# Eight cores, a linear-attention layer and a ternary-weight FFN: the weight pieces get one pool of eighteen buffers, twelve of them keep their piece, and VectorE shares the sums

## The chip, the cores and the metric

The program runs on all 8 cores of one Trainium2 chip. Each core computes one batch element of 4096 rows on its own, with its own copy of the weights. The time is device microseconds of the slowest core; a result is a median of runs. "Span" is the time from the first to the last instruction of one profiled execution.

## The reference, cut to what matters

One layer: linear attention with chunks of 64, then a feed-forward part whose two weight matrices are quantized to -1, 0, 1.

```python
x = x + layernorm(attn(layernorm(x), W_qkv, W_o))     # x: 8 x 4096 x 1024
x = x + layernorm(ffn(layernorm(x), w1, b1, w2, b2, gamma, beta))

def weight_quant(w):                       # w1: 4096 x 1024, w2: 1024 x 4096
    scale = 1.0 / clip(mean(abs(w)), EPS)
    return clip(round(w * scale), -1, 1), scale
def qlinear(x, w, b):                      # rows of x quantized to 8 bits
    return (xq @ wq.T) / (sx * sw) + b
def ffn(x): h = layernorm(x) * gamma + beta
            return qlinear(gelu(qlinear(h, w1, b1)), w2, b2)
```

The threshold of a matrix needs the mean of all its magnitudes, so no element can be quantized before the whole matrix has been read once. The matrix is then needed a second time.

## The kernel before

The 4096 rows are 32 tiles of 128. There are two phases, and in both each engine has its program written out by hand, with semaphores between the engines.

**Attention phase.** A loop over i from -1 to 31. In iteration t, TensorE does K, Q and V of tile t+1, scores and outputs of tile t and ends with `out_proj(t)` (L403), 16 matmuls of 512 columns. ScalarE turns PSUM results out (`k_out`, `q_out`, `y_out`, `kf_out`) and takes norms (`ln2_sd`, needed by VectorE's `x1`). VectorE does `ln1`, `x1` (L523, which empties the PSUM pair that the next scores use), `ln3`, `masks` (L541, before TensorE's `attend`), `k_sums`, `v_scaled` (L558, empties the pair that the next K uses). The normalized rows `h1t` are turned by a DMA transpose issued from SP (L980); there is one `h1t` buffer, so ScalarE's `h1` of a tile waits for the transpose of the tile before. Tiles are normalized two at a time, in even iterations. In the last two iterations VectorE also prepares FFN rows (`front_a`, `front_b`, L601 to L631), for which gamma and beta must be loaded (L1127, L1128, the last DMAs of POOL before the end of this phase).

**The weights, in the background of that phase.** w1 and w2 are cut into 32 pieces each of 128 x 1024 float32 (512 KB). Each piece is loaded twice: once for its sum of magnitudes ("sum"), once for quantization ("quant"). The list `plan[t]` says which of the 128 steps belong to iteration t: cost 1 for a sum, 1.75 for a quant, spread over iterations 0 to 29, in even iterations a little less. A sum is one ScalarE activation with accumulation (L887). A quant is: POOL's `below` (L1102, writes `lt`, two buffers), VectorE's `quant_piece` (L569, writes `wqt`, four buffers), a DMA transpose from SP into `w1p` or `w2p` (L987, L991). On ScalarE the first sum of an iteration stands before `y_out`, the rest at the iteration's end, ahead of the next `ln2_sd`. On VectorE, in odd iterations, the first quant stands before `masks`, the second before `v_scaled`, the rest behind it; in even ones the first before `v_scaled`, the rest behind it.

POOL issues the loads (L1123) in the order of the steps, at most four in flight, each after its buffer is free. Buffers before: eight in the space of `w1p` (`pc1`) for the 32 sums of w1, eight in the space of `w2p` (`pc2`) for the next 64 steps, then four for the rest (`pc` and two of `pc2`), two for the last six. For a quant POOL's order is `below(q-2)`, load of q, `below(q-1)`, load of q+1: a piece is asked for two steps ahead.

**FFN phase.** For each tile `ffn1` (L427, fp8 weights, 64 matmuls), then `ffn2` (L439, 64 matmuls), with gelu on ScalarE and quantization on VectorE.

## Time and profile before

| | |
|---|---|
| median of 3 runs | 1606.2 us (1605.7 to 1608.01) |
| the profiled execution's time | 1602.83 us |
| its span on the slowest core (core 2) | 1601.3 us, 1591.7 to 1601.3 over the cores |
| PE / DVE / ACT / POOL busy | 91% / 70% / 41% / 18% |
| attention phase, to the end of the last `out_proj` | to 685 us |
| FFN loop after it | from 709 us to the end |
| HBM read / written by the core | 119.03 MB / 33.55 MB |

Busy shares are means over two phases with different limits, so they are read by stage. TensorE is the engine with the most work in both; the time between two `out_proj` of neighbouring iterations shows what an iteration took.

### The profile page before, as it was taken

Reading aid. Unit: us, or ns where it says so; the run is one execution under the profiler, and the core shown is the slowest. Engines: PE = TensorE matmul, PEld = TensorE weight load, DVE = VectorE, ACT = ScalarE, POOL = GpSimd, SP = SyncE. Lnnn points to the kernel's source line nnn. Section 1 sums busy time; section 2 is a strip of 40 time slices with the busy share of each in tenths; the row PEclk is TensorE's granted clock in tenths of the full one; section 3 lists DMA queues with packets and bytes.
Section 4 is the critical chain, followed back from the end, with each engine's and each line's share of the span. In section 5 each row is a group of like instructions: output and inputs, shape, how many; then the busy total and the mean of one; then the engine's idle time right before and its main releaser. Section 6 shows DMA issues by size and latency. Waiting matters only on the chain.

```text
span 1601.3 us, 26580 instructions; the slowest of 8 cores (1591.7 to 1601.3 us)
## 1 busy us (share of the span) xinstructions
PE 1459.8 (91%) x8948; PEld 723.0 (45%) x8948; DVE 1116.3 (70%) x1861; ACT 662.8 (41%) x1057; POOL 282.3 (18%) x211
## 2 busy tenths in 40 slices
PE   0488599999999998689999999999999999999997
PEld 0245355655555555334444444444444444444443
DVE  3755356677777876676777767777677776767764
ACT  1078477677555655333323232232322323223231
POOL 1111124555667775000000000000000000000000
PEclk9989899999999999999999999999999999999999
DMA  9968868988889786243342543424334243342422
GB/s 192 294 162 250 195 160 203 215 228 230 188 188 214 197 180 159 90 89 79 81 100 61 107 74 81 100 61 111 71 82 98 60 111 71 89 92 60 103 52 66
DMA packets 285045, 209.94 MB, mean 131 GB/s; under 512 B 246632, under 2 KB 248680, under 8 KB 284912
## 3 DMA queue, kind: packets, MB, share of 16 engines
q1 hardware_dynamic: 261776, 131.16, 36.7%
q0 software_dynamic: 23136, 77.08, 18.1%
q8 instruction: 74, 1.21, 0.4%
q14 instruction: 59, 0.48, 0.1%
HBM read 119.03 MB, written 33.55 MB: 95 GB/s over the span
## 4 chain that ended last, share of the span: by engine, by line
PE 66%; DMA 12%; issue 7%; ACT 4%; DVE 4%; DVEq 3%; POOL 2%; SPq 2%; ACTq 1%; POOLq 0%
PE pz L439 28%; PE pp L427 27%; DMA pc<-w 7%; PE pp L317 4%; DMA h1f<-h1t 3%; PE pp L335 2%; PE pp L403 2%; POOL lt L1102 2%; DMA kst<-w_qkv 1%; PE pp L418 1%; ACT pc L887 1%; SPq L1007 1%; DVEq L725 1%; DVEq L512 1%; DVE wqtp L569 1%
## 5 line engine op out<-in xcount | busy, mean ns | idle before, releaser
L427 PE MATMUL pp<-w1p,xq1f 128*128 128x512 fp8e4 x2048 | 457.0, 381 | 0.0
L439 PE MATMUL pz<-w2p,xq2f 128*128 128x512 fp8e4 x2048 | 447.1, 379 | 0.0
L439 PEld LDWEIGHTS pz<-w2p,xq2f 128*128 128x128 bf16 x2048 | 200.4, 98 | 241.6
L427 PEld LDWEIGHTS pp<-w1p,xq1f 128*128 128x128 bf16 x2048 | 195.8, 98 | 243.9 <-issue 19.9
L638 DVE TENSOR_REDUCE st<-gsb 128x1 f32<-128x1024 f32 x128 | 152.6, 1214 | 130.6 <-ACT gsb L895 130.4
L901 ACT ACT_TABLE_LOAD x31 | 39.8, 1283 | 469.5 <-DVE st L677 469.5
L1102 POOL TENSOR_SCALAR lt<-pc,st 128x1024 bf16<-128x1024 f32 x64 | 192.5, 3008 | 143.6 <-DMA pc<-w 83.2
L895 ACT ACTIVATE gsb<-pp,st 128x1024 f32<-128x1024 f32 x128 | 142.1, 1110 | 104.5 <-PE pp L427 98.7
L317 PE MATMUL pp<-wk,h1f 128*128 128x512 bf16 x512 | 121.2, 389 | 68.9 <-DMA h1f<-h1t 33.2
L317 PE MATMUL pp<-wv,h1f 128*128 128x512 bf16 x512 | 125.8, 390 | 15.7 <-ACT kt L838 12.6
L1123 POOL DMA_DIRECT2D pc<-w x128 | 82.8, 647 | 215.7 <-ACT pc L887 115.0
L403 PE MATMUL pp<-wo,yf 128*128 128x512 bf16 x512 | 115.7, 379 | 1.2 <-ACT yf L867 1.2
L569 DVE SCALAR_TENSOR_TENSOR wqtp<-pc,st,lt 128x1024 fp8e4<-128x1024 f32 x64 | 85.7, 1346 | 37.9 <-POOL lt L1102 37.8
L317 PEld LDWEIGHTS pp<-wk,h1f 128*128 128x128 bf16 x512 | 50.7, 100 | 130.9 <-issue 77.5
L660 DVE TENSOR_SCALAR xq2t<-gsb 128x1024 bf16<-128x1024 f32 x128 | 88.8, 694 | 19.4 <-issue 1.5
L541 DVE TENSOR_TENSOR scT<-pp,mask 128x1024 bf16<-128x1024 f32 x64 | 75.3, 1218 | 35.9 <-PE pp L346 35.9
L655 DVE TENSOR_SCALAR gsb<-gsb,st 128x1024 f32<-128x1024 f32 x128 | 95.8, 749 | 2.8 <-issue 0.4
L317 PEld LDWEIGHTS pp<-wv,h1f 128*128 128x128 bf16 x512 | 47.3, 100 | 67.9 <-issue 22.7
L670 DVE SCALAR_TENSOR_TENSOR zb<-pz,st,b2b 128x512 f32<-128x512 f32 x64 | 47.9, 748 | 39.6 <-PE pz L439 39.6
L403 PEld LDWEIGHTS pp<-wo,yf 128*128 128x128 bf16 x512 | 48.7, 98 | 54.2 <-issue 1.3
L838 ACT CAST kt<-pp 128x512 bf16<-128x512 f32 x64 | 35.8, 582 | 76.8 <-PE pp L317 76.7
L335 PE MATMUL pp<-h1f,wqa 128*128 128x256 bf16 x512 | 60.2, 277 | 7.6 <-DMA h1f<-h1t 7.6
(114 smaller groups left out, 1511.5 us busy)
## 6 DMA issues: line engine op xcount, KB each, us to landing
pc<-w POOLq DMA_DIRECT2D x128, 512.0 KB, 5.9
xs<-x SPq DMA_DIRECT2D x32, 512.0 KB, 5.7
x1s<-xs SPq DMA_DIRECT2D x32, 512.0 KB, 4.6
xs<-x1s SPq DMA_DIRECT2D x32, 512.0 KB, 3.6
out<-xs SPq DMA_DIRECT2D x32, 512.0 KB, 3.1
wost<-w_o POOLq DMA_DIRECT2D x8, 512.0 KB, 49.3
kst<-w_qkv SPq DMA_DIRECT2D x8, 512.0 KB, 19.5
wv<-w_qkv POOLq DMA_DIRECT2D x1, 2048.0 KB, 31.6
```

Of the source, the lines that this page charges most:

```text
L317: mi = PE.matmul(half(n, h), lhsT=hf[:, kk, :], rhs=wt[:, kk, h * 512:(h + 1) * 512], start=(kk == 0), stop=(kk == 7))
L335: mi = PE.matmul(pair(n)[:, m * 256:(m + 1) * 256], lhsT=wt[:, kk, m * 128:(m + 1) * 128], rhs=hf[:, kk, :], start=(kk == 0), stop=(kk == ...
L403: mi = PE.matmul(half(n, h), lhsT=yf[:, kk, :], rhs=wo[:, kk, h * 512:(h + 1) * 512], start=(kk == 0), stop=(kk == 7))
L427: mi = PE.matmul(half(n, h), lhsT=xf[:, kk, :], rhs=w1q[:, kk % 4, c0:c0 + 512, kk // 4], start=False, stop=(kk == 7), skip_group_check=True)
L439: mi = PE.matmul(PZ[:, h * 512:(h + 1) * 512], lhsT=xq2f[:, t % 2, kk, :], rhs=w2q[:, kk % 16, h * 512:(h + 1) * 512, kk // 16], start=(kk ...
L569: V.scalar_tensor_tensor(out=wqt[:, j % 4].rearrange("p n e -> p e n"), in0=piece_buf(q)[0].rearrange("p (e n) -> p e n", e=2), scalar=c1( ...
L638: V.tensor_reduce(out=c1(amq, s), in_=gsb[:, s * 1024:(s + 1) * 1024], axis=AX.X, op=ALU.max, apply_absolute_value=True)
L655: V.tensor_scalar(out=g, in0=g, scalar1=s2, scalar2=M32, op0=ALU.mult, op1=ALU.add)
L660: V.tensor_scalar(out=xq2t[:, s * 1024:(s + 1) * 1024], in0=g, scalar1=M32, scalar2=None, op0=ALU.subtract).then_inc(s_xq2, 1)
L895: A.activation(out=gsb[:, s * 1024:(s + 1) * 1024], in_=pair(n)[:], func=AF.Gelu, scale=c1(dq1, t % 2)).then_inc(s_fr[n % 3], 2)
L1102: GP.tensor_scalar(out=lt[:, j % 2], in0=buf, scalar1=c1(nth, p[1]), scalar2=None, op0=ALU.is_lt).then_inc(s_lt, 1)
L1123: GP.dma_start(out=dst, in_=piece_src(p)).then_inc(s_ld, 16)
```

## The change

- **Layout.** `w1p` and `w2p` are laid out piece by piece: a transposed piece is 1024 bytes in a row of each partition. The moving operand of the FFN matmuls is then 4 blocks of 128 columns, where it was 512 columns in a row. TensorE waits for w2's transposes only before the first `ffn2`.
- **Buffers.** One pool of 18: two of `pc`, eight of `pc1`, eight of `pc2`. A buffer in the space of `w1p` or `w2p` may be used until the first piece that is written over it is quantized. Seven pieces of w1 and five of w2 stay in their buffer between sum and quant: 116 loads, where there were 128.
- **Order and time.** The pieces that stay are summed last. w2 is quantized in its plain order. The steps are spread over iterations 0 to 30, with 1.6 for a quant.
- **Sums.** VectorE takes 27 of the 64 sums (`piece_vsum`, a reduction of magnitudes), 17 of them of w1; ScalarE keeps 37.
- **POOL.** Before the step at place q of the list, POOL issues all loads whose buffer's last use is at place q-2 or earlier, then does `below` if the step is a quant.

```diff
-    w1p = at("w1p", O_W1, [4, HID], BF16)
-    w2p = at("w2p", O_W2, [16, D], BF16)
+    w1p = at("w1p", O_W1, [NWP, 4, 128], BF16)
+    w2p = at("w2p", O_W2, [8, 16, 128], BF16)
...
+    gap, hold = 12, (7, 5)
+    order = [list(range(hold[k], NWP)) + list(range(hold[k])) for k in range(2)]
...
-    line += [("quant", 1, 4 * c + b) for b in range(4) for c in range(8)]
-    cost = {"sum": 1.0, "quant": 1.75}
+    line += [("quant", 1, j) for j in range(NWP)]
+    cost = {"sum": 1.0, "quant": 1.6}
+    first, last = 0, T - 2
...
+    def on_dve(p):
+        return p[0] == "sum" and (p[2] < hold[p[1]]
+                                  or place[p] < NWP + gap and place[p] % 5 in (1, 3))
...
+    bufs = ([pc[:, k] for k in range(2)] + [pc1[:, k] for k in range(8)]
+            + [pc2[:, k] for k in range(8)])
+    covered = ([4 * NWP] * 2 + [place[("quant", 0, 4 * k)] for k in range(8)]
+               + [place[("quant", 1, 4 * k)] for k in range(8)])
+    held = [-1] * 10 + [8] * 8
...
+        z = min((b for b in own if end < covered[b]), key=lambda b: held[b])
...
-                                       rhs=w1q[:, kk % 4, c0:c0 + 512, kk // 4],
+                                       rhs=w1q[:, c0 // 128:c0 // 128 + 4, kk % 4, :, kk // 4],
...
-                                   rhs=w2q[:, kk % 16, h * 512:(h + 1) * 512, kk // 16],
+                                   rhs=w2q[:, 4 * h:4 * h + 4, kk % 16, :, kk // 16],
...
+        def piece_vsum(p):
+            buf, s_ld, landed = piece_buf(p)
+            V.wait_ge(s_ld, landed)
+            V.tensor_reduce(out=c1((acc1, acc2)[p[1]], p[2]), in_=buf, axis=AX.X, op=ALU.add,
+                            apply_absolute_value=True).then_inc(s_vabs, 1)
...
+            if p[2] % 4 == 0 and sums_under(p[1], p[2]) > 0:
+                SP.wait_ge(s_abs, sums_under(p[1], p[2]))
...
+        def load(n):
+            p = loads[n]
+            buf, s_ld, _ = piece_buf(p)
+            if n >= 4:
+                GP.wait_ge(piece_buf(loads[n - 4])[1], piece_buf(loads[n - 4])[2])
+            o, used = prior[p]
...
+            if used and pieces[o][0] == "quant":
+                GP.wait_ge(s_q, nqua[o] + 1)
...
+            GP.dma_start(out=buf, in_=piece_src(p)).then_inc(s_ld, 16)
...
         for q, p in enumerate(pieces):
...
+            while n < len(loads) and prior[loads[n]][0] <= q - 2:
+                load(n)
+                n += 1
+            if p[0] == "quant":
+                below(p)
```

## Rows read from the trace of the kernel before

**Rows 1.** Windows: the stages; time, busy of each engine, granted clock, DMA share, GB/s.

```profile
94.00:225.00 131.00, 105.12 (x871) 61.31 (x869) 59.10 (x107) 96.80 (x201) 21.41 (x36) 0.93 0.79 206
225.00:449.00 224.00, 214.72 (x1875) 128.25 (x1874) 161.75 (x251) 158.68 (x327) 119.54 (x81) 1.00 0.86 210
449.00:614.00 165.00, 151.28 (x1299) 90.03 (x1297) 128.15 (x187) 91.55 (x190) 110.13 (x58) 0.98 0.82 191
709.00:1602.00 893.00, 882.75 (x4210) 389.30 (x4208) 651.72 (x1139) 258.81 (x246) 0.00 (x0) 1.00 0.36 82
```

**Rows 2.** Timeline of PE: `out_proj` of iterations 0, 6, 13, 14, 19, 28, 30.

```profile
93.96 3.62 PE L403 MATMUL pp<-wo,yf 128*128 128x512 bf16 x16
...
224.77 3.62 PE L403 MATMUL pp<-wo,yf 128*128 128x512 bf16 x16
...
345.44 3.62 PE L403 MATMUL pp<-wo,yf 128*128 128x512 bf16 x16
361.77 3.62 PE L403 MATMUL pp<-wo,yf 128*128 128x512 bf16 x16
...
448.97 1.24 PE L403 MATMUL pp<-wo,yf 128*128 128x512 bf16 x5
...
614.00 3.62 PE L403 MATMUL pp<-wo,yf 128*128 128x512 bf16 x16
...
651.40 3.62 PE L403 MATMUL pp<-wo,yf 128*128 128x512 bf16 x16
```

**Rows 3.** Groups by line: costs of the operations that the change touches.

```profile
L1102 POOL TENSOR_SCALAR lt<-pc,st 128x1024 bf16<-128x1024 f32 x64 | 192.5, 3008 | 143.6 <-DMA pc<-w 83.2 <-DVE wqtp L569 59.6
...
L887 ACT ACTIVATE pc<-pc 128x1024 f32<-128x1024 f32 x64 | 67.0, 1050 | 0.0
...
L610 DVE TENSOR_REDUCE st<-h 128x1 f32<-128x1024 f32 x32 | 39.0, 1220 | 2.4
```

**Rows 4.** Timelines around iteration 5: POOL, ACT, then PE.

```profile
175.61 0.70 POOL L1123 DMA_DIRECT2D pc<-w  x1 [2.63 <-DMA pc<-w]
178.85 1.24 ACT L811 ACTIVATE h1t<-xs,st 128x1024 bf16<-128x1024 f32 x1 [11.27 <-DMA h1f<-h1t]
182.16 5.36 PE L317 MATMUL pp<-wk,h1f 128*128 128x512 bf16 x16 [9.85 <-DVE vt L558]
192.21 5.32 PE L335 MATMUL pp<-h1f,wqa 128*128 128x256 bf16 x32 [4.69 <-DMA h1f<-h1t]
```

**Rows 5.** One line's view: transposes of h1 (L980), then of xq2 (L1076), to landing.

```profile
DMA to landing us min/median/max: 3.0/5.3/16.9
...
DMA to landing us min/median/max: 3.0/3.4/5.0
```

**Rows 6.** Timelines, iterations 19 and 20: POOL, then DVE.

```profile
452.68 2.83 POOL L1102 TENSOR_SCALAR lt<-pc,st 128x1024 bf16<-128x1024 f32 x1 [3.23 <-DMA pc<-w]
455.68 2.82 DVE L569 SCALAR_TENSOR_TENSOR wqtp<-pc,st,lt 128x1024 fp8e4<-128x1024 f32 x1 [4.25 <-POOL lt L1102]
460.10 1.41 DVE L523 SCALAR_TENSOR_TENSOR xs<-pp,st,xs 128x512 f32<-128x512 f32 x2
```

**Rows 7.** Timelines, iteration 29 to the first FFN matmul: DVE, POOL, PE.

```profile
630.04 1.27 DVE L569 SCALAR_TENSOR_TENSOR wqtp<-pc,st,lt 128x1024 fp8e4<-128x1024 f32 x1
641.65 1.29 DVE L569 SCALAR_TENSOR_TENSOR wqtp<-pc,st,lt 128x1024 fp8e4<-128x1024 f32 x1 [4.67 <-POOL lt L1102]
652.73 1.16 DVE L601 SCALAR_TENSOR_TENSOR h<-xs,st,gam 128x1024 f32<-128x1024 f32 x1
638.64 2.84 POOL L1102 TENSOR_SCALAR lt<-pc,st 128x1024 bf16<-128x1024 f32 x1 [3.12 <-DMA pc<-w]
662.80 0.61 PE L418 MATMUL pp<-b1r,xq1f 4*128 4x512 bf16 x2 [7.78 <-DMA xq1f<-xq1t]
```

**Rows 8.** Landing: piece loads (L1123) from 600 to 640 us, then beta's.

```profile
DMA to landing us min/median/max: 4.4/5.4/6.6
...
bet<-beta POOLq DMA_DIRECT2D x1, 512.0 KB, 5.3
```

More of the change, by code:

```diff
@@ L222, in build @@
     s_S = sem("state_out")
[L223 to L226 removed]
+    s_pl = [sem(f"piece_loaded{i}") for i in range(18)]
+    s_abs, s_vabs = sem("piece_summed"), sem("piece_summed_by_dve")
+    s_lt, s_q = sem("piece_lt"), sem("piece_quantized")
     s_wtp = [sem(f"piece_transposed{i}") for i in range(4)]
@@ L253, in build @@
         spent += cost[p[0]]
-    last_sum = [max(i for i in range(T) if ("sum", k, NWP - 1) in plan[i]) for k in range(2)]
+    last_sum = [max(i for i in range(T) if ("sum", k, NWP - 1) in plan[i]
+                    or ("sum", k, hold[k] - 1) in plan[i]) for k in range(2)]
     assert all(p[0] == "sum" or last_sum[p[1]] + 2 <= i for i in range(T) for p in plan[i])
@@ L258, in build @@
     place = {p: q for q, p in enumerate(pieces)}
-    nsum = [sum(1 for p in pieces[:q] if p[0] == "sum") for q in range(len(pieces))]
-    nqua = [sum(1 for p in pieces[:q] if p[0] == "quant") for q in range(len(pieces))]
-    early = 3 * NWP
-    def piece_buf(q):
-        if q < NWP:
-            return pc1[:, q % 8], s_wl1[q % 8]
-        if q < early:
-            return pc2[:, q % 8], s_wld[q % 8]
-        z = (q - early) % 4 if q < early + 24 else (q - early) % 2
-        return (pc[:, z] if z < 2 else pc2[:, 4 + z]), s_wll[z]
@@ new lines, in build @@
+    nsum = [sum(1 for p in pieces[:q] if p[0] == "sum" and not on_dve(p))
+            for q in range(len(pieces) + 1)]
+    nvsum = [sum(1 for p in pieces[:q] if on_dve(p)) for q in range(len(pieces) + 1)]
+    nqua = [sum(1 for p in pieces[:q] if p[0] == "quant") for q in range(len(pieces) + 1)]
+    bufs = ([pc[:, k] for k in range(2)] + [pc1[:, k] for k in range(8)]
+            + [pc2[:, k] for k in range(8)])
+    covered = ([4 * NWP] * 2 + [place[("quant", 0, 4 * k)] for k in range(8)]
+               + [place[("quant", 1, 4 * k)] for k in range(8)])
@@ new lines, in build @@
+    held = [-1] * 10 + [8] * 8
+    count = [0] * 18
+    loads, where, prior = [], {}, {}
+    for p in pieces:
+        if p[0] == "quant" and p[2] < hold[p[1]]:
+            where[p] = where[("sum", p[1], p[2])]
+            continue
+        stays = p[0] == "sum" and p[2] < hold[p[1]]
+        end = place[("quant", p[1], p[2])] if stays else place[p]
+        own = range(2 + 8 * p[1], 10 + 8 * p[1]) if stays else range(18)
+        z = min((b for b in own if end < covered[b]), key=lambda b: held[b])
+        count[z] += 1
+        where[p] = (z, 16 * count[z])
+        prior[p] = (held[z], count[z] > 1)
+        held[z] = end
+        loads.append(p)
@@ L288, in q_of, with piece_buf, sums_under @@
+    def piece_buf(p):
+        return bufs[where[p][0]], s_pl[where[p][0]], where[p][1]
+    def sums_under(k, z):
+        under = [place[p] for p in pieces
+                 if p[0] == "sum" and not on_dve(p) and where[p][0] == 2 + 8 * k + z // 4]
+        return nsum[max(under)] + 1 if under else 0
     def q_of(t, j):
@@ L495, in pe_program @@
                 ffn1(t + 1, [2, 3])
+            if t == 0:
+                for k in range(4):
+                    PE.wait_ge(s_wtp[k], 16 * 2 * NWP // 4)
             ffn2(t)
@@ L574, in quant_piece, with take_piece @@
                                    saturate=False).then_inc(s_q, 1)
+        def take_piece(p):
+            if p[0] == "sum":
+                piece_vsum(p)
+            else:
+                quant_piece(p)
         def w_total(k):
-            V.wait_ge(s_abs, NWP * (k + 1))
+            V.wait_ge(s_abs, nsum[max(place[("sum", k, j)] for j in range(NWP)) + 1])
+            V.drain()
             V.tensor_reduce(out=c1(tot, k), in_=(acc1, acc2)[k], axis=AX.X,
@@ L743, in dve_program @@
                     w_total(k)
-            now = [p for p in plan[t] if p[0] == "quant"] if 0 <= t < T else []
+            now = [p for p in plan[t] if p[0] == "quant" or on_dve(p)] if 0 <= t < T else []
             if two:
@@ L766, in dve_program @@
             for p in now[done:done + 1]:
-                quant_piece(p)
+                take_piece(p)
             if u < T:
@@ L937, in act_program @@
                 gelu(0, 1)
-            now = [p for p in plan[t] if p[0] == "sum"] if t >= 0 else []
+            now = [p for p in plan[t] if p[0] == "sum" and not on_dve(p)] if t >= 0 else []
             for p in now[:1]:
```

87 lines of the change are left out of this document (29 added, 58 removed).

## The prediction

> **What bounds the kernel now.** I read the stages first [rows 1]. From 709 us TensorE is busy 882.75 of 893 us at full granted clock: the FFN loop is TensorE's own time, and only the speed of its matmuls can change it. Before that, from 94 to 225 us, TensorE is busy 105 of 131 us at a mean clock of 0.93, while ScalarE is busy 97; from 225 to 449 it is nearly full; from 449 to 614 it loses 14 us, with VectorE at 128 of 165. So what the change can win lies in the first and the third stretch of the attention phase.
>
> The steps between two `out_proj` say it more exactly [rows 2]. Iteration 14 took 361.77 - 345.44 = 16.33 us, the least that I saw, and several took just that: TensorE without a wait. Against it: iterations 1 to 6 took 224.77 - 93.96 = 130.8, six times 16.33 is 98.0, so 32.8 us are lost. Iterations 7 to 19: 224.2 against 212.3, 11.9 lost. 20 to 28: 165.0 against 147.0, 18.1 lost. 29 and 30: 37.4 against 32.7, 4.7 lost.
>
> The early loss has two parts. Iteration 5 alone was 18 us late. Before it POOL had asked for w2's first pieces into eight untouched buffers, four always in flight, to 175.61 [rows 4]. The h1 transposes beside them took up to 16.9 us where the median is 5.3 [rows 5]; ScalarE sat 11.27 us for the one `h1t` buffer, and TensorE 9.85 and 4.69 [rows 4]. The matmuls behind the waits are also slow: 16 of them in 5.36 us, where `out_proj` has 16 in 3.62. The rest, some 9 us in iterations 1 to 4, is ScalarE: five or seven sums of 1.05 us [rows 3] in each iteration, four to six of them ahead of `ln2_sd`, so `x1` and `k_out` come late.
>
> The loss of 20 to 28 is mostly of one kind [rows 6]: POOL waits for a piece that was asked for only two steps ahead (3.23 us), VectorE waits for POOL's `lt` (4.25), and `x1` of the next iteration starts at 460.10, some 9 us after its `out_proj` allowed it. `lt` waited 83.2 us for loads in all [rows 3].
>
> **The change part by part**, against the profiled execution of 1602.8 us; the median of the runs is 3.4 above it, and I carry the difference over.
>
> *Sums to VectorE, spread of loads (iterations 1 to 6).* ScalarE keeps 3, 4, 3, 3, 2, 1 sums in iterations 0 to 5, where it had 5, 7, 5, 7, 5, 7. `ln2_sd` then comes 2 to 5 us sooner. VectorE gets 17 reductions of w1, of about 1.22 us each (the magnitude maximum over the same shape, [rows 3]), 2 to 3 in an iteration of 16, 6 in iteration 5. VectorE is busy 59 of 131 us there [rows 1], so 21 us more fit: one in odd iterations lies ahead of `masks`, but `x1` has moved up by more. That takes away nearly all of the 9 us. The loads: walking the list, the untouched buffers are now met in groups of 10 at the start, 6 behind the sum at place 8 (iteration 1) and 2 behind place 18 (iteration 3), the last with four more whose buffers are free by then. So two bursts of about 9 loads stand where one of 13 stood, ending near the h1 transposes of iterations 2 and 4. The last four loads of a burst, 2 MB, need about 2 MB / 206 GB/s = 10 us at the stage's rate [rows 1], against the 5.3 us that a transpose may take. I take 3 us lost at the first burst, 6 at the second, 3 elsewhere, 12 in all: a gain of 32.8 - 12 = **20**. Bounds: 29 if the bursts do no harm (some 4 us of threshold and pairing waits stay), 5 if the transposes stall as before and only part of ScalarE's 9 us comes back.
>
> *Middle (7 to 19).* As many ScalarE sums per iteration as before; five VectorE sums for the kept w2 pieces fall into iterations 15 to 17, where VectorE then has 4, 3 and 5 pieces: about 16 us of work in the even one, just its length. Against this stand deeper loads. **0**, from -5 to +5: the loss there is 11.9, and either side can take some of it.
>
> *Deeper loads (20 to 28).* A load now goes out as soon as its buffer's last use is two places back, which puts it 2 to 8 places ahead of its quant up to place 121. `lt` then waits only for VectorE: the fourth piece of an odd iteration is ready about 0.5 + 0.8 + 3 us after the second is quantized, and VectorE gets to it after about 4. So the waits of [rows 6] go. Of 18.1 lost I leave 4 (slow h1 transposes, even iterations with three pieces): gain **14**, from 8 to 17.
>
> *The end of the list.* This is the part that costs. w2's transposes cover its buffers as they go, and the last pieces have only the two `pc` buffers and one more. The loads of places 124 to 127 find their buffer's last use exactly two places back, so they are issued at their own place, directly before `below` waits for them: nothing is fetched ahead. Before, at places 122 to 127, a `below` stood between. The list also ends one iteration later: 121 to 124 in iteration 29, 125 to 127 in iteration 30, where before there was none. Iteration 30 is also where VectorE, behind its last quant, prepares the first FFN rows, and TensorE already waits for these: its first FFN matmul comes at 662.80 after 7.78 us idle [rows 7].
>
> Let X be the end of iteration 29's second quant (630.04 + 1.27 = 631.3 before). Before, the rows were begun at 652.73 and the FFN at X + 31.5. After: the load of 124 waits for X, plus 0.5 to wake; landing takes 4.4 to 6.6 us, median 5.4 [rows 8]; I take 4.9, since one is in flight and not two; `below` takes 2.84 to 3.0 [rows 3, 7]. Four such steps follow each other on POOL: X + 0.5 + 4 x (4.9 + 2.9) = X + 31.7. Quant 127 ends at about X + 33. But gamma and beta are asked for only behind POOL's last `below`: + 0.6 for the first issue + 5.3 for beta to land [rows 8] = X + 37.6, which is later. From there the rows and their transpose take what they took, 662.80 - 652.73 = 10.1: X + 47.7. That is 16.2 later than X + 31.5. `masks(30)`, held up behind quant 125 by some 3 us, lies inside that wait. **Cost 16**, from 14 (landing 4.4) to 23 (landing 6.6). If it were covered by nothing else being late it would be zero, but TensorE was already idle at this place, so every microsecond counts.
>
> *Layout.* Zero for the transposes: turned rows with stepped destinations (h1) and with unbroken ones (xq2) both take 3.0 us at least [rows 5]. The Trainium skill, "DMA: Bandwidth & Descriptors", section "Latency and other measured facts", says that a transpose with a non-contiguous middle dimension runs at 261 GB/s where a contiguous one has 350 to 400; by that the pieces' transposes would be a third shorter. The rows above do not agree, and no wait for a piece's transpose is among them, so the sum is the same by either. For the FFN matmuls, no row has a moving operand in four blocks of 128. From below nothing excludes a cost; I take zero, because 64 matmuls' worth of stepped fp8 columns already run with TensorE always busy [rows 1]. A gain is excluded, since it is never idle there.
>
> 12 loads fewer, 6 MB of 119 and 12 issues of 0.65 us, are inside the terms above. SP's new waits for sums are long met; VectorE's added drain in `w_total` is one of two.
>
> **Sum:** -20 + 0 - 14 + 16 + 0 = -18. Profiled time 1602.8 - 18 = 1585; median 1606.2 - 18 = **1588**.
>
> **The rivals.**
> - *The transposes stall as before (0.15).* The DMA share is 0.79 already in this stretch [rows 1], and the same megabytes come sooner. Then the early gain is 5: -5 - 14 + 16 = -3, about 1603, at best just faster. The Trainium skill, same page, section "Issuing engines are not separate DMA queues", says that DMAs from all engines share 16 engines and interleave, so that a transpose is behind whatever POOL has asked for. The 16.9 us in [rows 5] agrees. The rule counts what is in flight, and that stays at four.
> - *VectorE becomes the bound (0.10).* It waits in order for pieces to land, ahead of `masks` and `x1`, and at 97% in iterations 16 and 17. Half of the early gain goes and 5 us in the middle: -10 + 5 - 10 + 18 = +3, about 1609. Against it: early loads run at least ten places ahead of their sum.
> - *The four-block operand slows the FFN (0.07), slower.* There are 63 x 64 = 4032 such matmuls in 893 us, 221 ns each. From 18 us / 4032 = 4.5 ns more (2%) the gain is gone; at 10 ns the time is 1588 + 40 = 1628. For it speaks only that no row shows such an operand; against it, that the blocks are still 256 bytes in a row.
> - *The end costs little (0.08).* If the last loads land in 4.4 and iteration 29 runs earlier than I allow, +12 and -32: about 1573. The chain on POOL speaks against less.
>
> **How the numbers follow.** My own case has 0.60, 1575 to 1600. A difference within 0.2% (3.2 us) can't be told from none here. Faster: 0.60 + 0.08 + two thirds of the first rival (0.09) + a third of the second (0.03) = 0.80. Within 0.2%: 0.05 + 0.03 = 0.08. Slower: 0.07 + 0.04 + 0.01 = 0.12. The range goes from 1571 (early gain 27, deeper loads 17, end 14: -30, with some room below) to 1607 (the first rival with an end of 20).
>
> **What would show it.** Right: iterations 1 to 4 at about 17 us, iteration 5 no longer 34; h1 landings at most 10 us; no wait of L569 for `lt` in iterations 20 to 28; piece loads of places 124 to 127 each followed by a wait of POOL for them, VectorE idle in iteration 30, and TensorE idle some 20 us before its first FFN matmul; the FFN loop as long as before. Wrong: an FFN loop longer than 893 us, transposes of 15 us beside bursts, or VectorE waiting for loads in iterations 1 to 5.

## The result, and the profile after

The changed kernel takes **1627.2 us** (median of 4 runs, 1625.0 to 1638.5), the kernel before, beside it, 1607.1 (4 runs, 1605.7 to 1608.1): a ratio of **1.014, 95% interval 1.0092 to 1.0188**. It is 20 us slower. The forecast was 1588, range 1571 to 1607: wrong in sign, and outside the range. The profiled execution took 1624.97 us.

In some executions half of the chip's cores run at a lower granted clock: such executions are left out of the times, and where it touched the profiled one (wait_seven_back and h1_turned_first, some of cores 4 to 7, 0.86 to 0.93 in the middle), the middle is read on cores 0 to 3. The kernel before took 1602.5, 1605.9 and 1603.0 us beside the three groups of experiments.

The page of the kernel after: the span, the engines' busy times, the traffic, both FFN matmuls, and POOL's `below`.

```profile
span 1623.4 us, 26481 instructions; the slowest of 8 cores (1609.6 to 1623.4 us)
...
PE 1460.7 (90%) x8884; PEld 726.6 (45%) x8948; DVE 1149.8 (71%) x1888; ACT 637.3 (39%) x1003; POOL 271.7 (17%) x199
...
HBM read 112.74 MB, written 33.55 MB: 90 GB/s over the span
...
L444 PE MATMUL pp<-w1p,xq1f 128*128 128x512 fp8e4 x2048 | 457.0, 382 | 0.0
L456 PE MATMUL pz<-w2p,xq2f 128*128 128x512 fp8e4 x2048 | 447.1, 380 | 0.0
...
L1135 POOL TENSOR_SCALAR lt<-pc,st 128x1024 bf16<-128x1024 f32 x64 | 188.5, 2946 | 44.5 <-DMA pc<-w 22.8
```

The wait of `below` for loads fell from 83.2 us [rows 3] to 22.8, and 6 MB less were read. The kernel is slower all the same. Windows of the kernel after, core 2, cut at the same `out_proj` as [rows 1]; columns as there.

```profile
94.00:225.00 131.00, 104.06 (x862) 61.25 (x872) 80.50 (x126) 79.24 (x163) 20.53 (x34) 0.90 0.79 196
225.00:467.00 242.00, 217.18 (x1835) 130.79 (x1860) 168.15 (x255) 149.23 (x308) 104.41 (x68) 0.96 0.73 177
467.00:617.00 150.00, 147.58 (x1285) 89.02 (x1302) 127.45 (x187) 92.66 (x191) 102.43 (x53) 1.00 0.79 187
617.00:704.00 87.00, 54.02 (x394) 29.15 (x395) 45.52 (x69) 29.02 (x56) 29.69 (x16) 0.84 0.42 107
704.00:1623.00 919.00, 906.84 (x4313) 399.39 (x4314) 672.17 (x1168) 268.91 (x260) 0.53 (x1) 1.00 0.37 83
```

ScalarE was relieved in the first stretch (79 us busy, 97 before [rows 1]) and the stretch is as long as it was. The second is longer with a clock of 0.96 where it was 1.00; the third is shorter; the fourth has TensorE busy 54 of 87 us. From the start of the last `out_proj` to the end of the span it is 919.1 us on core 2, before 919.7: the FFN part is as long as it was.

The yardstick for all that follows is the time between the starts of two `out_proj` in the timeline of PE, as in [rows 2], here as a mean over the 8 cores of each kernel's profiled execution. Kernels in which a stretch is untouched differ there by up to 3.5 us, 5 in the middle; a step ("step 9" is the time from `out_proj` of iteration 8 to that of iteration 9) is a mean of the 8 cores too.

| us, mean of 8 cores | 1 to 6 | 7 to 19 | 20 to 28 | 29 to 31 | start of last `out_proj` |
|---|---|---|---|---|---|
| before | 129.3 | 225.2 | 161.2 | 66.3 | 676.8 |
| after | 129.4 | 237.9 | 150.0 | 85.3 | 696.2 |
| forecast of the difference | -20 | 0 | -14 | +16 | -18 |
| measured | +0.1 | +12.7 | -11.2 | +19.0 | +19.4 |
| two_in_flight | 104.3 | 236.9 | 150.1 | 83.9 | 668.2 |
| two_in_flight_old | 119.3 | 232.3 | 160.3 | 66.2 | 671.0 |
| two_in_flight_not_shared | 113.0 | 233.6 | 151.6 | 85.9 | 678.5 |
| wait_seven_back | 129.3 | 232.6 | 149.6 | 85.8 | 690.7 |
| h1_turned_first | 131.6 | 239.1 | 148.9 | 83.5 | 696.4 |
| tail_prefetched | 132.8 | 241.4 | 150.1 | 75.0 | 693.5 |
| list_ends_at_29 | 132.0 | 240.3 | 159.3 | 75.6 | 701.9 |
| all_three_mended | 103.9 | 228.5 | 149.5 | 75.1 | 651.9 |
| mended_two_throughout | 106.8 | 223.5 | 151.7 | 74.9 | 649.8 |
| mended_threshold_odd | 106.1 | 231.3 | 151.1 | 74.1 | 656.1 |
| layout_only | 129.4 | 224.7 | 158.9 | 65.9 | 672.2 |
| old_list_to_30 | 112.2 | 222.2 | 157.1 | 78.4 | 663.1 |

**The first stretch.** Steps 1 to 6 took 16.3, 16.4, 29.2, 16.3, 30.8 and 20.4 us, where they were 17.8, 19.7, 19.0, 19.7, 31.6 and 21.3. Timelines of the kernel after, core 2: POOL's loads, then ScalarE, then TensorE.

```profile
111.85 2.23 POOL L1154 DMA_DIRECT2D pc<-w  x4 [4.93 <-ACT pc L918]
...
126.64 0.53 POOL L1154 DMA_DIRECT2D pc<-w  x1 [1.65 <-DMA pc<-w]
...
154.51 2.03 POOL L1154 DMA_DIRECT2D pc<-w  x3 [2.86 <-DVE st L586]
...
182.04 0.72 POOL L1154 DMA_DIRECT2D pc<-w  x1 [5.02 <-DMA pc<-w]
...
136.91 1.24 ACT L843 ACTIVATE h1t<-xs,st 128x1024 bf16<-128x1024 f32 x1 [12.19 <-DMA h1f<-h1t]
...
183.96 1.24 ACT L843 ACTIVATE h1t<-xs,st 128x1024 bf16<-128x1024 f32 x1 [13.95 <-DMA h1f<-h1t]
...
140.21 5.14 PE L334 MATMUL pp<-wk,h1f 128*128 128x512 bf16 x16 [10.87 <-DVE vt L578]
...
187.27 5.50 PE L334 MATMUL pp<-wk,h1f 128*128 128x512 bf16 x16 [12.71 <-DVE vt L578]
```

The h1 transposes issued at 118.89 and 163.68 us, inside the two bursts, landed after 17.9 and 20.2 us, with 3.4 and 3.8 piece loads in flight beside them on the mean (on the eight cores, 17.2 to 20.2 us). So the picture of [rows 4] is there twice. One line's view of the h1 transposes of the kernel after (L1011), issue to landing, from 60 to 130 and from 130 to 180 us:

```profile
DMA to landing us min/median/max: 3.4/5.9/17.9
...
DMA to landing us min/median/max: 3.1/11.7/20.2
```

**The middle.** Of its +12.7 us, 9.3 are step 9 (26.8, before 17.5) and 5.5 step 18 (21.8, before 16.3); others go up and down by up to 2.3. Waits of the kernel after, core 2, 222 to 467 us: in total, times, longest.

```profile
POOL pc L1154 <- DVE wqtp L594: 66.2, 14, 12.4
POOL pc L1154 <- ACT pc L918: 58.3, 9, 16.4
POOL pc L1154 <- DVE st L586: 11.2, 1, 11.2
...
PE pp L352 <- DMA h1f<-h1t: 18.4, 5, 7.2
```

Before, POOL's waits there were the 68.4 us of `below` for loads; to free a buffer it waited 10.8, and TensorE waited 0.2 for h1. Timelines of step 9 (core 2): POOL, VectorE, ScalarE, SP, TensorE.

```profile
262.42 0.70 POOL L1154 DMA_DIRECT2D pc<-w  x1 [11.17 <-DVE st L586]
263.16 2.85 POOL L1135 TENSOR_SCALAR lt<-pc,st 128x1024 bf16<-128x1024 f32 x1
...
260.66 1.20 DVE L586 TENSOR_REDUCE st<-pc 128x1 f32<-128x1024 f32 x1
...
263.78 1.23 DVE L578 TENSOR_TENSOR vt<-pp,st 128x1024 bf16<-128x1024 f32 x1
266.12 1.29 DVE L594 SCALAR_TENSOR_TENSOR wqtp<-pc,st,lt 128x1024 fp8e4<-128x1024 f32 x1 [1.11 <-POOL lt L1135]
...
261.85 1.24 ACT L843 ACTIVATE h1t<-xs,st 128x1024 bf16<-128x1024 f32 x1 [0.74 <-DMA h1f<-h1t]
...
267.54 1.20 SPq L1020 DMA_TRANSPOSE w1p<-wqtp  x1
268.88 1.40 SPq L1011 DMA_TRANSPOSE h1f<-h1t  x1
...
276.42 5.32 PE L352 MATMUL pp<-h1f,wqa 128*128 128x256 bf16 x32 [7.24 <-DMA h1f<-h1t]
```

POOL stood 11.17 us at a *load*, for a VectorE sum two places back, while the piece of the `below` behind it had landed: `below` ran 0.04 us after the load was out, without a wait. The experiments below start from this theory: for this reason `lt`, the quant, and the piece's transpose on SP came late one after the other, and the h1 transpose, which stands behind that one on SP, came late with them. The lines bear out only the last link. The second h1 of the pair was ready at 263.09 us and its transpose was issued at 268.88, behind the piece's. But VectorE waited for `lt` only 1.11 us (0.4 on the mean of the cores). The quant is late by VectorE's own order: iteration 8 is even, its list begins with a VectorE sum (L586), and that sum takes the place before `v_scaled` (L578), so the quant runs behind it. It is the only even iteration with quants whose list begins so.

Means of the eight cores, at step 9: how long after its h1 the second h1 transpose was issued, how long it took to land, and the step.

| us | issued late by | landed in | step 9 |
|---|---|---|---|
| before | 0.2 | 4.1 | 17.5 |
| after | 5.0 | 7.7 | 26.8 |
| two_in_flight | 5.0 | 5.9 | 27.1 |
| wait_seven_back | 5.2 | 4.6 | 22.3 |
| all_three_mended | 4.8 | 3.2 | 22.5 |
| mended_two_throughout | 4.8 | 4.3 | 21.7 |
| two_in_flight_not_shared (no such sum) | 2.1 | 5.2 | 18.8 |
| h1_turned_first (h1 first on SP) | 0.1 | 6.3 | 19.8 |
| list_ends_at_29 (no such sum) | 0.1 | 6.8 | 21.9 |
| mended_threshold_odd (no such sum) | 0.9 | 8.9 | 22.0 |

The landings matter too, and that of the pair's first h1 transpose: 7.7 us in the kernel after, 11.0 in two_in_flight and all_three_mended, 10.2 in list_ends_at_29. So a transpose issued in time is not enough, as the last two rows show.

**The end.** Timelines from the last but one `out_proj`, core 2: POOL, VectorE, TensorE.

```profile
635.04 0.76 POOL L1154 DMA_DIRECT2D pc<-w  x1
642.03 2.83 POOL L1135 TENSOR_SCALAR lt<-pc,st 128x1024 bf16<-128x1024 f32 x1 [6.24 <-DMA pc<-w]
...
649.81 2.83 POOL L1135 TENSOR_SCALAR lt<-pc,st 128x1024 bf16<-128x1024 f32 x1 [4.22 <-DMA pc<-w]
...
658.39 2.83 POOL L1135 TENSOR_SCALAR lt<-pc,st 128x1024 bf16<-128x1024 f32 x1 [5.03 <-DMA pc<-w]
...
666.44 2.83 POOL L1135 TENSOR_SCALAR lt<-pc,st 128x1024 bf16<-128x1024 f32 x1 [4.49 <-DMA pc<-w]
...
669.84 0.55 POOL L1167 DMA_DIRECT2D bet<-beta  x1
...
675.27 0.17 DVE L632 MEMSET xq1t<- 128x128 bf16 x1 [4.54 <-DMA bet<-beta]
...
685.37 0.61 PE L435 MATMUL pp<-b1r,xq1f 4*128 4x512 bf16 x2 [21.31 <-DMA xq1f<-xq1t]
```

This is the chain that the forecast describes, four times load, wait, `below` (only the first of the four loads is shown), and then beta. TensorE is idle 21.3 us, where it was 7.78 [rows 7].

### The profile page after: what moved, and what is told of

It reads as the page before. It is cut to its first block, busy times and chain, and to the rows that moved or that the text cites. A ratio compares the mean times of both kernels' runs of the same rounds, so it can differ in the third digit from the quotient of the medians.

```text
span 1623.4 us, 26481 instructions; the slowest of 8 cores (1609.6 to 1623.4 us)
## 1 busy us (share of the span) xinstructions
PE 1460.7 (90%) x8884; PEld 726.6 (45%) x8948; DVE 1149.8 (71%) x1888; ACT 637.3 (39%) x1003; POOL 271.7 (17%) x199
## 4 chain that ended last, share of the span: by engine, by line
PE 75%; DMA 9%; DVE 4%; issue 4%; DVEq 3%; ACT 2%; SPq 2%; POOL 1%; ACTq 0%; POOLq 0%
PE pz L456 27%; PE pp L444 27%; PE pp L334 7%; PE pp L352 6%; DMA h1f<-h1t 5%; PE pp L420 4%; DMA pc<-w 2%; DMA kst<-w_qkv 1%; PE pp L435 1%; POOL lt L1135 1%; SPq L1040 1%; DVEq L757 1%; DVEq L532 1%; DVE wqtp L594 1%; PE pp L363 1%
## 5 line engine op out<-in xcount | busy, mean ns | idle before, releaser
L444 PE MATMUL pp<-w1p,xq1f 128*128 128x512 fp8e4 x2048 | 457.0, 382 | 0.0
L456 PE MATMUL pz<-w2p,xq2f 128*128 128x512 fp8e4 x2048 | 447.1, 380 | 0.0
L444 PEld LDWEIGHTS pp<-w1p,xq1f 128*128 128x128 bf16 x2048 | 195.9, 98 | 243.8 <-issue 19.7
L1135 POOL TENSOR_SCALAR lt<-pc,st 128x1024 bf16<-128x1024 f32 x64 | 188.5, 2946 | 44.5 <-DMA pc<-w 22.8
L1154 POOL DMA_DIRECT2D pc<-w x116 | 75.1, 648 | 353.2 <-ACT pc L918 105.2
L334 PE MATMUL pp<-wv,h1f 128*128 128x512 bf16 x465 | 114.6, 389 | 6.5 <-issue 2.8
L692 DVE TENSOR_SCALAR xq2t<-gsb 128x1024 bf16<-128x1024 f32 x128 | 88.9, 694 | 19.4 <-issue 1.5
L352 PE MATMUL pp<-h1f,wqa 128*128 128x256 bf16 x512 | 66.7, 295 | 18.9 <-DMA h1f<-h1t 18.9
```

What stands on the lines that cost most here:

```text
L334: mi = PE.matmul(half(n, h), lhsT=hf[:, kk, :], rhs=wt[:, kk, h * 512:(h + 1) * 512], start=(kk == 0), stop=(kk == 7))
L352: mi = PE.matmul(pair(n)[:, m * 256:(m + 1) * 256], lhsT=wt[:, kk, m * 128:(m + 1) * 128], rhs=hf[:, kk, :], start=(kk == 0), stop=(kk == ...
L444: mi = PE.matmul(half(n, h), lhsT=xf[:, kk, :], rhs=w1q[:, c0 // 128:c0 // 128 + 4, kk % 4, :, kk // 4], start=False, stop=(kk == 7), skip ...
L456: mi = PE.matmul(PZ[:, h * 512:(h + 1) * 512], lhsT=xq2f[:, t % 2, kk, :], rhs=w2q[:, 4 * h:4 * h + 4, kk % 16, :, kk // 16], start=(kk == ...
L692: V.tensor_scalar(out=xq2t[:, s * 1024:(s + 1) * 1024], in0=g, scalar1=M32, scalar2=None, op0=ALU.subtract).then_inc(s_xq2, 1)
L1135: GP.tensor_scalar(out=lt[:, j % 2], in0=buf, scalar1=c1(nth, p[1]), scalar2=None, op0=ALU.is_lt).then_inc(s_lt, 1)
```

## The experiments

Each is the kernel after with the edit shown, unless it says otherwise. Ratios are to the kernel before, run beside it.

**two_in_flight**: of the first 45 loads only two are in flight.

```diff
-            if n >= 4:
-                GP.wait_ge(piece_buf(loads[n - 4])[1], piece_buf(loads[n - 4])[2])
+            w = 2 if n < 45 else 4
+            if n >= w:
+                GP.wait_ge(piece_buf(loads[n - w])[1], piece_buf(loads[n - w])[2])
```

> The changed kernel, with at most two piece loads in flight instead of four among the first 45 loads. Burst theory: the turned rows h1 take 18 and 20 us because four 512 KB loads of the same core are always queued beside them, and that is why iterations 3 and 5 take 28.9 and 31.1 us. Then no h1 transpose before 230 us lands later than about 10 us, and the six steps from out_proj 0 to out_proj 6 take 105 to 113 us where the changed kernel takes 129.7; time 1627 - 20 = about 1607. Rival, total traffic: the slow transposes come from all the chip's traffic, however deep this core's queue is; the same bytes move in the same stretch, so landings stay above 15 us and the stretch above 122. Rival, VectorE's sums: it waits for pieces to land; then fewer loads in flight make it longer, above 130.

1601.0 us, ratio 1.0001 (0.9967 to 1.0034). Steps 1 to 6 fell from 129.4 to **104.3**, step 3 to 18.0 and step 5 to 17.5; the other stretches moved by 1.4 us at most. The same view as above, from 60 to 130 and from 130 to 180 us, core 2 of this kernel:

```profile
DMA to landing us min/median/max: 4.9/5.3/6.5
...
DMA to landing us min/median/max: 4.2/5.7/7.3
```

On the other cores landings go up to 11.0 us. The two transposes that took 17.2 to 20.2 us in the kernel after take 5.9 to 10.6 here, over all cores. The bursts cost 25 us, more than the 20 that the change should have won there. Total traffic, the rival, is excluded: landings and stretch both fell.

**two_in_flight_old**: the same limit in the kernel *before*.

```diff
-                GP.wait_ge(piece_buf(q - 4)[1], piece_landed(q - 4))
+                w = 2 if q < 45 else 4
+                GP.wait_ge(piece_buf(q - w)[1], piece_landed(q - w))
```

> The kernel before, with the same limit of two loads in flight for its first 45 places. Burst theory: its one late iteration (34.6 us, 18 late) goes too, and the first six steps take 112 to 118 us instead of 130.8; ScalarE's part of the loss (9 us) stays; 1607 - 15 = about 1592. Total traffic: unchanged, 128 to 133.

1603.0 us, ratio 0.9998 (0.9957 to 1.004). Step 5 went from 31.6 to 20.9 and the stretch by -10, to 119.3, just outside what was expected. But 7 to 19 took 7 us more, for which no run gives a cause, and the time did not move. That the old burst has the same cause is shown; that removing it pays in the old kernel is not.

**two_in_flight_not_shared**: two_in_flight, and VectorE sums only the pieces that stay.

```diff
-        return p[0] == "sum" and (p[2] < hold[p[1]]
-                                  or place[p] < NWP + gap and place[p] % 5 in (1, 3))
+        return p[0] == "sum" and p[2] < hold[p[1]]
```

> The changed kernel with two loads in flight among the first 45, as in the run of that name, and in addition VectorE sums only the twelve pieces that stay in their buffers; ScalarE sums all others. It prices the sharing alone, with the bursts gone. ScalarE's theory: iterations 1 to 4 get their 1.5 to 3.5 us back each, so the six first steps take 112 to 119 us, where the shared version took 104.3 (mean of cores) and the kernel before with two in flight 119.3. If the gain of 15 between those two came from the order of the loads and not from ScalarE, it stays at 104 to 108.

1611.7 us, ratio 1.0027 (1.0005 to 1.0049). Steps 1, 2 and 4 are 17.8, 18.5 and 18.5 (16.4, 16.4 and 16.3 with the sums shared; 17.8, 19.7 and 19.7 before the change), and the stretch is 113.0. So the sharing of the sums is worth 113.0 - 104.3 = **8.7 us**, once the bursts don't hide it. The same edit takes the VectorE sum out of iteration 8, and step 9 falls from 27.1 to 18.8.

**wait_seven_back**: up to place 84, a load goes out only when its buffer's last use is seven places back, so that its wait is met sooner.

```diff
-            while n < len(loads) and prior[loads[n]][0] <= q - 2:
+            while n < len(loads) and prior[loads[n]][0] <= q - (7 if q < 85 else 2):
```

> The changed kernel, but up to place 84 POOL issues a load only when its buffer's last use is seven or more places back, not two. Theory of the queue on POOL: in iterations 7 to 18 a load that waits for a sum or quant just two places back stands before below, so lt, the quant, its transpose on SP and, behind that, the h1 transpose come late. Then POOL's waits at the load line in 222 to 467 us (66 for quants, 58 for ScalarE sums, 11 for VectorE sums) fall under 30, TensorE's wait for h1 (18.4) under 6, and the 13 steps from out_proj 6 to 19 take 228 to 234 instead of 244.5; time about 1614. Rival, the bursts or the number of VectorE pieces: the stretch stays at 240 or more.

1620.3 us, ratio 1.0101 (1.0057 to 1.0146), which overlaps the kernel after's: a gain in time is not shown by it alone. On cores 0 to 3 the middle took 229.2 us, against 239.9 on the same cores of the kernel after. Step 9 went from 26.8 to 22.3, step 18 from 21.8 to 19.0. Waits of POOL, and of TensorE for h1, core 2, 222 to 460 us:

```profile
POOL lt L1135 <- DVE wqtp L594: 103.2, 16, 14.4
...
POOL pc L1154 <- DVE st L586: 21.6, 1, 21.6
...
POOL pc L1154 <- ACT pc L918: 16.4, 3, 12.1
...
PE pp L352 <- DMA h1f<-h1t: 12.8, 3, 8.4
POOL pc L1154 <- DVE wqtp L594: 10.6, 3, 7.6
```

POOL now waits at `below`, for its own `lt` buffer, and less at loads: 48.6 us in all, where it was 135.7. That is not under the 30 that was expected, and TensorE's wait for h1 is 12.8 and not under 6. VectorE waits 0.2 us for `lt` here, and yet the second h1 transpose of step 9 is issued as late as before the edit (5.2 us). So a late `lt` was not what held it. What fell there is its landing, from 7.7 to 4.6 us, since the loads now go out at other times. In step 18 VectorE no longer waits for `lt` (1.3 us in the kernel after, before its first quant), and there POOL's order may be the cause of the 2.8 us. The edit moves the loads and frees `below` at once, and no run separates the two.

**h1_turned_first**: on SP the h1 transpose is issued before the iteration's first piece transpose.

```diff
-            for p in now[:1]:
-                piece_tp(p)
             if two:
                 h1_tp(f + 1)
-            for p in now[1:]:
+            for p in now:
                 piece_tp(p)
```

> The changed kernel, but in even iterations SP issues the second h1 transpose before the first piece transpose, not behind it. If POOL's late lt does its harm through SP's queue, TensorE's wait for h1 between 222 and 467 us (18.4) falls under 8 and the steps 6 to 19 take 230 to 236 instead of 244.5, with POOL's own waits as they were; time about 1616. If it does its harm through VectorE waiting for lt (14.0 us there), the stretch stays above 240. If the h1 transposes themselves are slow, it also stays above 240, with landings of 7 us and more.

1633.0 us (1619.2 to 1634.1), ratio 1.0167 (1.0108 to 1.0225): no gain in time is shown. Step 9 fell from 26.8 to 19.8, and to 16.5 to 19.6 on seven of the eight cores, where it was 24.5 to 30.5. TensorE's wait for h1 in the middle fell from 18.4 to 7.2 us on core 2. The table's 239.1 for the middle is the mean of all cores; on cores 0 to 3 it took 234.2 us (222.0 to 252.7), against 239.9, as the first case of the expectation has it, but with a spread that leaves the size open. POOL still waited 76.7 and 36.3 us at loads for VectorE's quants and ScalarE. So with those waits as they were, the order of SP alone gave back 7 of the 9.3 us of step 9.

**list_ends_at_29**: the steps are spread over iterations 0 to 29, as before.

```diff
-    first, last = 0, T - 2
+    first, last = 0, T - 3
```

> The changed kernel, with the list of steps spread over iterations 0 to 29, as before, and not to 30; loads and their order as in the changed kernel, so the last four are still issued directly before they are needed. Theory of the end: the chain of four load-then-below steps (about 8.5 us each) then runs in iterations 28 and 29, and gamma and beta land before they are needed. The three steps from out_proj 28 to 31 take 68 to 72 us where the changed kernel takes 85.3 (mean of the cores) and the kernel before 66.3; time about 1627 - 15 = 1612. Rival: it is the missing prefetch alone, wherever it lies; then the three steps stay at 80 or more. The first two stretches may be up to 5 us longer, since odd iterations get five pieces.

1630.7 us, ratio 1.0143 (1.0113 to 1.0172). The end won 10 us (75.6, not the 68 to 72 that was expected), but 20 to 28 lost 9: **159.3**, nearly the 161.2 of before, with the deep loads in place. VectorE's wait for `lt` was 7.8 us in that stretch on core 2, and the stretch was long all the same.

**tail_prefetched**: from place 121 on, a load goes out one place after its buffer's last use, and gamma and beta are asked for before the last `below`.

```diff
-            while n < len(loads) and prior[loads[n]][0] <= q - 2:
+            while n < len(loads) and prior[loads[n]][0] <= q - (1 if q >= 121 else 2):
...
+            if q == 127:
+                GP.wait_ge(s_Q, 2 * (T - 1))
+                GP.dma_start(out=gam[:], in_=gamma_h.partition_broadcast(128)).then_inc(s_gbl[0], 16)
+                GP.dma_start(out=bet[:], in_=beta_h.partition_broadcast(128)).then_inc(s_gbl[1], 16)
             if p[0] == "quant":
                 below(p)
```

> The changed kernel, list to iteration 30 as it stands, but from place 121 on a load is issued one place earlier (its buffer's last use one place back suffices), and gamma and beta are asked for ahead of the last below. Theory of the end: each of the last steps has its landing beside a below, the last quant ends some 6 us earlier, and gamma and beta are there: out_proj 28 to 31 in 68 to 74 us instead of 85.3, time about 1613. Rival: with quants left in iteration 30 the stretch stays above 80, because the FFN's first rows stand behind them on VectorE.

1622.3 us, ratio 1.0095 (1.0067 to 1.0123). 29 to 31 fell from 85.3 to 75.0, a little less than expected: of the 19 us that the end costs, 10 are the loads issued at their own place and beta behind the last `below`.

**all_three_mended**: the edits of two_in_flight, wait_seven_back and tail_prefetched together.

> Three changes at once on the changed kernel: two loads in flight among the first 45; up to place 84 a load waits only for uses seven or more places back; from place 121 on one place back, with gamma and beta ahead of the last below. If the three losses are separate and add up: 104 + 232 + 150 + 71 us for the four stretches, last out_proj at about 651 us against 676.8 before and 696.2 in the changed kernel (means of the cores), and a time of 1607 - 26 = about 1581. If they are the same lost time seen at three places, above 1595.

**1583.4 us, ratio 0.9859 (0.9826 to 0.9892)**: 23 us faster than the kernel before. The stretches are 103.9, 228.5, 149.5 and 75.1; the three losses are separate and come off one by one. Its windows, core 2, cut at the same `out_proj`:

```profile
94.00:196.00 102.00, 97.32 (x851) 58.89 (x861) 77.54 (x124) 76.03 (x157) 17.03 (x30) 1.00 0.88 225
196.00:425.00 229.00, 214.69 (x1805) 127.95 (x1829) 165.61 (x254) 151.55 (x310) 104.49 (x73) 0.98 0.83 197
...
575.00:650.00 75.00, 55.85 (x416) 30.27 (x419) 45.26 (x66) 31.27 (x60) 28.97 (x16) 0.86 0.59 135
```

The first stretch now has a DMA share of 0.88 and 225 GB/s, more than the 0.79 and 196 of the kernel after: two loads in flight move the bytes no slower, over the stretch, than four.

**mended_two_throughout**: all_three_mended with two in flight for all loads (`w = 2`).

> The run with all three mended, with two loads in flight throughout instead of only among the first 45. In that run iteration 9 still took 22.5 us (17.5 in the kernel before), behind a load group sent out just before an h1 transpose once four were allowed again. If the burst is the cause there too, iteration 9 falls to 17 to 19, steps 6 to 19 from 228.5 to 222 to 226, and the time from 1583 to about 1578. If the queue on POOL is what is left, nothing changes, or it gets longer since loads are later: 228 to 235.

**1577.1 us, ratio 0.9856 (0.9829 to 0.9882)**, against a kernel before of 1603.0. By the ratios the same as all_three_mended; the middle is 223.5 in its profile, 5 less, no more than two profiles may differ by there. Step 9 is 21.7 and not 17 to 19: four loads in flight were not the main thing that kept it long. The second h1 transpose is still issued 4.8 us late.

**mended_threshold_odd**: mended_two_throughout with w2's last sum in an odd iteration again.

```diff
-    gap, hold = 12, (7, 5)
+    gap, hold = 13, (7, 5)
...
-    cost = {"sum": 1.0, "quant": 1.6}
+    cost = {"sum": 1.0, "quant": 1.75}
```

> As the run with two loads throughout, but with the sums of w2 ending one iteration earlier (13 pieces ahead instead of 12, cost 1.75 instead of 1.6 in the plan), so that w2's threshold is taken in iteration 17, an odd one, as in the kernel before, and not in iteration 18, where VectorE also normalizes two tiles. Iteration 18 took 21.8 us in the changed kernel, 16.3 before. If this placement is the cause: iterations 17 and 18 together 34 to 35 us instead of 38 and a time 3 to 4 us lower. If it is VectorE's five pieces in iteration 17: no change in the sum.

1582.6 us, ratio 0.987 (0.9844 to 0.9897). Step 18 is 17.2 (18.8 without the edit) but 17 is 18.8 (17.5), so that the two together are 36.0 and were 36.3. The place of the threshold is worth nothing that can be measured. The middle is 231.3, 7.8 longer; the edit moves many steps to other iterations, and no run says which of them costs this.

**layout_only**: the kernel *before* with the new layout of `w1p` and `w2p` and w2's plain order.

```diff
-    line += [("quant", 1, 4 * c + b) for b in range(4) for c in range(8)]
+    line += [("quant", 1, j) for j in range(NWP)]
...
-                                       rhs=w1q[:, kk % 4, c0:c0 + 512, kk // 4],
+                                       rhs=w1q[:, c0 // 128:c0 // 128 + 4, kk % 4, :, kk // 4],
```

> The kernel before with the new layout of the two quantized matrices alone (and w2 quantized in plain order, which this layout needs); buffers, loads, sums and list as before. My prediction priced the layout at zero. Then: FFN from the last out_proj to the end as before (919.7 us on core 2), piece transposes landing in 2.4 to 2.5 us at least, and 1607 within 3. If a contiguous destination made the transposes a third shorter, their median falls from 5 to under 4 us, with no effect on the time.

1604.3 us, ratio 1.0006 (0.9977 to 1.0035). Its FFN matmuls, by line, core 2:

```profile
L427 PE MATMUL pp<-w1p,xq1f 128*128 128x512 fp8e4 x2048 | 457.3, 382 | 0.0
L439 PE MATMUL pz<-w2p,xq2f 128*128 128x512 fp8e4 x2048 | 447.1, 379 | 0.0
```

Before they took 457.0 and 447.1. Transposes of w1's pieces landed in 2.5/4.8/9.2 us (least, median, most), before in 2.4/5.2/9.7; w2's in 2.4/4.9/10.0, before 2.4/4.6/8.2. The layout is worth nothing either way, by the time and by the matmuls.

**old_list_to_30**: the kernel *before*, with a quant at 1.6 and the steps spread over iterations 0 to 30.

```diff
-    cost = {"sum": 1.0, "quant": 1.75}
-    share = sum(cost[p[0]] for p in line) / (T - 2)
+    cost = {"sum": 1.0, "quant": 1.6}
+    share = sum(cost[p[0]] for p in line) / (T - 1)
...
-        while i < T - 3 and spent >= share * (i + (1.0 if i % 2 else 0.8)):
+        while i < T - 2 and spent >= share * (i + (1.0 if i % 2 else 0.8)):
```

> The kernel before, with its list spread over iterations 0 to 30 at cost 1.6 as in the changed kernel; its own buffers, loads and sums. It asks whether the 11 us won in steps 19 to 28 come from deeper loads, as I predicted, or from the wider spread of the list. Deeper loads: the stretch stays at 157 to 162 us (161.2 before, 150.0 changed). Wider spread: it falls to 150 to 153. Either way the end grows, since three quants now stand before the first FFN rows: 66.3 to 72 to 78.

**1591.1 us, ratio 0.9941 (0.9924 to 0.9959)**: this part of the change alone makes the old kernel 0.6% faster. 20 to 28 took 157.1, at the edge of what was expected if the deeper loads do it, and 29 to 31 took 78.4. The surprise is the first stretch, 112.2: step 5 took 16.7 us on the mean of the cores, where it was 31.6, with buffers, order and four in flight as they were. Timelines, core 2: POOL's burst, then SP's h1 transposes next to it.

```profile
169.34 2.73 POOL L1123 DMA_DIRECT2D pc<-w  x4 [6.30 <-ACT pc L887]
...
191.44 0.70 POOL L1123 DMA_DIRECT2D pc<-w  x1 [4.23 <-DMA pc<-w]
...
166.00 1.25 SPq L980 DMA_TRANSPOSE h1f<-h1t  x1
...
195.10 1.36 SPq L980 DMA_TRANSPOSE h1f<-h1t  x1
```

The burst goes out wholly between two h1 transposes. In the kernel before the transpose of 161.86 us fell into it. So a burst did harm where it met a transpose, and this one, which met none, cost nothing that shows.

## Why the prediction was wrong, point by point

**What bounds the kernel.** Right: the gain was to be had in the first and third stretch, and the FFN loop is TensorE's own time.

**Sums to VectorE and the loads, -20, measured +0.1: failed.** Half of the step holds: the sharing is worth 8.7 us, where the forecast had "nearly all of the 9". The other half is the mis-sized term "3 us lost at the first burst, 6 at the second". Against 16.33, steps 3 and 5 lost 12.9 and 14.5 us; with two in flight 1.7 and 1.2. The forecast drained four loads, 2 MB in 10 us. But four stay in flight as long as a burst goes on, since each that lands is replaced: the two transposes met 8 and 9 loads and landed in 17.9 and 20.2 us. The row for it was there, 16.9 us beside the old burst [rows 5], and was argued down because the new bursts were shorter. One burst became two, each long enough to span a transpose. The rival that the transposes stall as before (5 us of gain left) was nearer than the forecast, and still too mild. The Trainium skill, "DMA: Bandwidth & Descriptors", section "Issuing engines are not separate DMA queues", says that transfers of all issuing engines interleave on the same 16 DMA engines; the landings with four and with two in flight agree.

**Middle, 0 from -5 to +5, measured +12.7: failed.** The step looked for VectorE's sums in iterations 15 to 17 alone, where they cost nothing (16 and 17 took 16.3 and 16.4), and put the rest at nothing. It overlooked the one VectorE sum at the head of iteration 8. That sum takes the quant's place before `v_scaled`, and SP issues an h1 transpose only behind that quant's. The transpose was issued 5.0 us late (0.2 before) and landed in 7.7 us (4.1 before), which is 8.4 of the 9.3 us of step 9. Two runs undo the first part each in its way, and step 9 is then 18.8 (no such sum) and 19.8 (h1 first on SP). In two others the sum is gone from there by another list, but the landings are long, and the step is 21.9 and 22.0.

The step also said of the loads that they go out when the last use is "two places back", and did not ask who waits while POOL waits for that use. Before, the load ahead of a `below` was of a buffer used eight places back, or four. wait_seven_back and all_three_mended give back 9 to 11 of the 12.7. How, is open in part: VectorE's wait for `lt` in the middle was 14.0 us, but 11.8 before the change too, so a late `lt` explains little of the difference; the landings of step 9 fell, and 2.8 us of step 18 may be POOL's. The threshold in an even iteration costs nothing that shows. Step 9 keeps 22.5 us in all_three_mended, with the transpose issued 4.8 us late; why the landings there differ from list to list, no run tells.

**Deeper loads, -14 within 8 to 17, measured -11.2: right in size, wrong in cause.** The waits of [rows 6] did go: VectorE's for `lt` fell from 15.4 to 4.0 us. But list_ends_at_29 has deep loads and a stretch of 159.3, old_list_to_30 has the old loads and 157.1; only both together give 150.0. Either alone is worth 2 to 4 us, hardly more than two profiles differ by. The forecast gave all to the loads, and took the spread over one more iteration into account only as a cost.

**The end, +16 within 14 to 23, measured +19.0: right.** The chain has each link that was named. TensorE's first FFN matmul came at 685.37, with iteration 29's second quant ended at 632.4 on core 2: X + 53.0, forecast X + 47.7. From a load's issue to its `below` it took 5.8 us on the mean and not 4.9 (0.76 us of issue and the waits of 6.24, 4.22, 5.03, 4.49), four times. And the first of the four loads went out 2.7 us behind X and not 0.5, since POOL was in the `below` of the piece before until then. From the kernels with either edit undone: ending in iteration 30 with the old loads costs 12 (66.3 to 78.4), the new rule of loads with the old end 9 (66.3 to 75.6).

**Layout, 0: right**, for the matmuls and for the time. The same page of the Trainium skill, section "Latency and other measured facts", gives 261 GB/s for a transpose with a non-contiguous middle dimension and 350 to 400 for a contiguous one. By these figures a piece of 128 KB would take some 0.50 us and 0.33 to 0.37, an estimate: 0.13 to 0.17 us of a landing of 2.4, and not a third of it, as the forecast had it. layout_only (2.5 and 2.4 us at least) shows no gain, but so small a one could hide in its landings.

**Rivals.** VectorE as the bound did not come: iterations 16 and 17, where it was to be 97% busy, took 16.3 and 16.4 us. The four-block operand did not slow the FFN. The end did not cost little.

**Slips in the working.** `x1` at 460.10 is not "some 9 us" but some 6.4 behind what allowed it, ScalarE's last step for its norm, which ended at 453.74. The last rival's sum does not come out: with an end of +12 the terms give -22, about 1584, not 1573. Two thirds of 0.15 are 0.10, not 0.09. None of them touches the steps that failed.

**The sum as measured:** 0.1 + 12.7 - 11.2 + 19.0 = 20.6 us, and the first `out_proj` 1.3 sooner: 19.4 at the last one, 20 in the median. The range was too narrow because two of four terms had bounds drawn around the forecast's own mechanism, not around the row of before.

## What to carry to other kernels

A limit on transfers in flight is a bound on how late a small transfer beside them lands. Where a short transfer is on the path (here a transpose behind a single buffer), look at every place where buffers come free in a group, and ask what will be issued beside it. When side work gets a new kind of step, check whose place it takes in every iteration, and what stands behind that one on other queues: one reduction moved a quant by one place, and through SP's fixed order it cost TensorE some 5 us. A prefetch that must wait for a buffer holds up what stands behind it on the same queue (POOL stood 11.17 us at one), so ask whether that work is ready. A side job's spread over one more iteration can be worth as much as a better order in it; price both its relief and its end.
